# Two semaphore waits fewer on GpSimd in the scan stage of a recurrent-mix and slot-attention kernel

## The chip, the cores and the metric

The kernel runs on 1 core of one Trainium2 chip. The metric is the device time of one execution in microseconds (us), taken as a median over runs. The engines are named as the profile names them: PE is TensorE (PEld its weight loads), DVE is VectorE, ACT is ScalarE, POOL is GpSimd, SP is SyncE, whose queue carries the DMAs.

## The reference

Four sequences of 1024 steps and 1024 channels go through a two-way exponential-decay scan, then through two rounds of a slot-attention block. Only the scan part is touched by the change. In it, with k = v = the side input and r = x:

```python
decay = exp(-exp(w)) * (0.5 + 0.5 * tf)          # per sequence and channel
ek = exp(min(k, 30)); ekv = ek * v
# forward and backward over the steps: a = a * decay + ekv ; b = b * decay + ek
num = nf + nb - ekv + exp(min(u + k, 30)) * v
den = df + db - ek + exp(min(u + k, 30))
x0 = sigmoid(r) * (num / max(den, 1e-8)) * (0.8 + 0.2 * tf)
```

x0 then goes through the two rounds of normalisation, top-4 selection per slot, attention over 16 slots and output projection, and is added to x at the end.

## The kernel before

The scan stage works on 32 tiles (NT), one for each of 4 sequences and 8 groups of 128 channels; a tile is 128 partitions (channels) by 1024 steps in fp32, even steps in the first half of the columns and odd ones in the second. Each engine has one instruction stream written out by hand; the streams are tied by counting semaphores, `wait(engine, sem, count)`. A producer adds 1 to its semaphore for each instruction.

For tile i, in the order of the data:

- SP loads k into kbuf (two buffers) and r into rbuf (three). Line 230, the load of k for tile n + 2, waits for ekv_ok and euv_ok of tile n.
- POOL L347 writes min(k, 30) into ek (two buffers), a tensor_scalar.
- ACT L263 takes exp of ek in place (ek_ok).
- DVE L294 and L296 (the helper `halves`) join neighbouring steps of ek into gfk: each is a scalar_tensor_tensor on 512 columns that reads two halves of a tile in SBUF. They count prek_ok, two for each tile. DVE L302 and L305 (the helper `scans`) are the forward and the backward scan of gfk; their decay factor is in PSUM.
- POOL L351 is ekv = ek * k, a tensor_tensor of two SBUF tiles into the one buffer ekv. DVE L294 and L296 then run again, from ekv into gfv (prev_ok), and L302 and L305 again on gfv.
- ACT L283 makes eu = exp(u + k); DVE L330 makes euv from eu and kbuf, both in SBUF (euv_ok); DVE L334 adds eu and the PSUM sum to den (den_ok).
- PE (helper line L368) adds up the two scans in PSUM: 4 matmuls for num (num_ok), 4 for den (sumk_ok), 2 for euv. L391 transposes x0 and L405 makes logit sums.
- The quotient is taken in logarithms: ACT L276 and L278 on den (l2_ok), ACT L271 exp(-r) on rbuf, POOL L354 a cap on it (tensor_scalar, in place), ACT L287 its logarithm (l1_ok), POOL L360 the sum of the two (tensor_tensor, both inputs in SBUF, s_ok), ACT L246 the exp of it (y_ok), and DVE L325 multiplies it with num from PSUM.

DVE's order in iteration n is: halves of gfk(n), scans of gfk(n), halves of gfv(n), L325 of tile n - 1, L330(n), L334(n), scans of gfv(n). In the texts "halves of gfk" are L294 and L296 on ek, and "halves of gfv" the same lines on ekv. POOL's order in iteration i is L347(i), L351(i), L354(i), L360(i - 1). ACT's order in iteration i: L246(i - 2), L250(i - 3), L260(i), L263(i), L267(i - 2), L271(i), L276(i - 1), L278(i - 1), L283(i), L287(i).

Before the change, POOL L351(i) waits for three counts: ek_ok (ACT L263 of tile i), prev_ok (both halves of gfv of tile i - 1, which have read ekv), and euv_ok (DVE L330 of tile i - 1). POOL L360(i - 1) waits for l1_ok, l2_ok and for prek_ok of tile i, that is for the halves of gfk that DVE runs in iteration i.

Of the kernel before, what the change touches and what calls it, by code (L numbers as in the profile page):

```python
# [16 lines left out]
NT = B * NC  # L17
# [12 lines left out]
def wait(eng, sem, count):  # L30

    if not (isinstance(count, int) and count <= 0):
        eng.wait_ge(sem, count)
# [20 lines left out]
def build(nc, xT, kT, x, cond, w_cols, u_cols, work_t, cw_cols, npre_cols, cb_col, wr_T, wr_b, wq, wk_T,  # L54
          wv_T, bq_cols, bk_cols, bv_cols, wo_T, wo_b, npost, out):
    with ExitStack() as ctx:
# [56 lines left out]
        def csem(name):  # L113
            cond_sems.append(cond_ctx.enter_context(nc.semaphore(name)))
            return cond_sems[-1]
# [19 lines left out]
        def constants_pool(pool):  # L135

            nc.gpsimd.memset(ident[:], 0.0).then_inc(c_id, 1)
            nc.gpsimd.memset(fold[:], 0.0).then_inc(c_id, 1)
            nc.gpsimd.memset(ones_row, 1.0).then_inc(c_id, 1)
            pool.wait_ge(c_id, 3)  # L140
            nc.gpsimd.affine_select(out=ident[:], in_=ident[:], compare_op=ALU.not_equal, fill=1.0, base=0,
                                    pattern=[[-1, P]], channel_multiplier=1).then_inc(c_id, 1)
            for q in range(Q):
                nc.gpsimd.affine_select(out=fold[:], in_=fold[:], compare_op=ALU.not_equal, fill=1.0,
                                        base=-32 * q, pattern=[[-1, S]], channel_multiplier=1).then_inc(c_id, 1)
                pool.wait_ge(c_id, 5 + q)
# [64 lines left out]
        dg_ok, ekv_ok, euv_ok = csem("diag_ok"), csem("ekv_ok"), csem("euv_ok")  # L211
        prek_ok, prev_ok, gfk_ok, gfv_ok = csem("prek_ok"), csem("prev_ok"), csem("gfk_ok"), csem("gfv_ok")
# [5 lines left out]
        with nc.Block() as block:  # L218
            @block.sync
            def _(sp):  # L220
                constants_sp(sp)
                for n in range(NT):
                    p = n % 2
                    if n > 0:
                        wait(sp, x0_ok, n)
                        sp.dma_start(x0T_d[n - 1, :, :], x0T).then_inc(x0_out, 16)
                    if n + 2 < NT:
                        wait(sp, ekv_ok, n + 1)
                        wait(sp, euv_ok, n + 1)
                        sp.dma_start(kbuf[p], kT[n + 2, :, :]).then_inc(k_in[p], 16)  # L230
                    if n + 3 < NT:
                        wait(sp, s_ok, n + 1)
                        sp.dma_start(rbuf[n % 3], xT[n + 3, :, :]).then_inc(r_in[n % 3], 16)
                wait(sp, x0_ok, NT)
                sp.dma_start(x0T_d[NT - 1, :, :], x0T).then_inc(x0_out, 16)
                sp.wait_ge(x0_out, 16 * NT)
# [101 lines left out]
            @block.gpsimd  # L338
            def _(pool):
                constants_pool(pool)  # L340
                for i in range(NT + 1):
                    p = i % 2
                    if i < NT:
                        wait(pool, k_in[p], (i // 2 + 1) * 16)
                        wait(pool, prek_ok, 2 * (i - 1))
                        wait(pool, ekv_ok, i - 1)
                        nc.gpsimd.tensor_scalar(ek[p], kbuf[p], EXP_MAX, None, ALU.min).then_inc(kc_ok, 1)  # L347
                        wait(pool, ek_ok, i + 1)
                        wait(pool, prev_ok, 2 * i)
                        wait(pool, euv_ok, i)  # L350
                        nc.gpsimd.tensor_tensor(ekv, ek[p], kbuf[p], ALU.mult).then_inc(ekv_ok, 1)  # L351
                        r = rbuf[i % 3]
                        wait(pool, er_raw, i + 1)
                        nc.gpsimd.tensor_scalar(r, r, ER_CAP, None, ALU.min).then_inc(er_ok, 1)  # L354
                    if i > 0:
                        n = i - 1
                        wait(pool, l1_ok, n + 1)
                        wait(pool, l2_ok, n + 1)
                        wait(pool, prek_ok, 2 * min(i + 1, NT))
                        nc.gpsimd.tensor_tensor(den[n % 2], den[n % 2], rbuf[n % 3], ALU.add).then_inc(s_ok, 1)  # L360

            @block.tensor
# [808 lines left out]
```

## Time and profile before

| | before |
|---|---|
| median of 3 runs | 1146.97 us (1146.0 to 1147.72) |
| the profiled execution's own time | 1146.0 us |
| its span, first to last instruction | 1144.2 us |
| mean granted TensorE clock | 0.984 of full |
| scan stage | from the start to about 404 us |
| DVE busy from 200 to 300 us | 98.19 us |
| POOL busy from 200 to 300 us | 87.45 us |

The time lies 1.8 us above the span, for what is before the first and after the last instruction. The scan stage is the first 404 us, in which all engines work on 32 tiles in a pipeline with a fixed rhythm; the two rounds of attention follow. In a timeline row an instruction has its start, its duration, and in brackets how long its engine had been idle before it and what ended that idle time. Successive DVE instructions overlap by some 0.08 us in such rows: a start-to-start distance is that much shorter than the duration.

### The profile page before, as it was taken

The page shows a single profiled execution, that of the slowest core. Times are in us where ns is not written, and L with a number is a line of the kernel's source. Part 1 is how long each engine was busy: PE and PEld are TensorE (multiplying, and loading weights), DVE is VectorE, ACT ScalarE, POOL GpSimd, SP SyncE. Part 2 cuts the span into 40 slices and gives each one's busy share as a digit, 9 for nine tenths or more (in the row PEclk, how much of TensorE's full clock was granted, in tenths as well). Part 3 has the DMA queues.
Part 4 walks back from the last instruction along what each step waited for, and adds up shares of the span by engine and source line. Part 5 has one row for each costly group of instructions (what it writes and reads, how often), then busy time and mean ns, then how long its engine had stood idle before and what let it go on. Part 6 is the DMA issues. An engine that isn't in the chain of part 4 may idle for free. (4 is left out here: it accounts for less than half of the span.)

```text
span 1144.2 us, 15666 instructions
## 1 busy us (share of the span) xinstructions
PE 1060.2 (93%) x5040; PEld 587.0 (51%) x5040; DVE 782.6 (68%) x1018; ACT 595.5 (52%) x972; POOL 447.3 (39%) x204
## 2 busy tenths in 40 slices
PE   2999999999999978989999999998889899999996
PEld 1443434434344432646666666665326466666663
DVE  6999999999999832365665666655223666666664
ACT  4778787887877720245555555555202433333332
POOL 6889888898888600001111111111000023333333
PEclk9999999999999989999999999999799999999998
DMA  3343343433434174953345354331659656778764
GB/s 132 117 148 122 129 147 114 154 119 128 148 113 151 50 276 177 361 189 110 111 137 176 114 175 141 110 110 74 248 219 342 203 192 224 277 242 278 244 219 148
DMA packets 83392, 196.54 MB, mean 172 GB/s; under 512 B 6802, under 2 KB 48914, under 8 KB 80276
## 3 DMA queue, kind: packets, MB, share of 16 engines
q1 hardware_dynamic: 83348, 195.97, 48.9%
q8 instruction: 25, 0.41, 0.2%
q14 instruction: 19, 0.16, 0.0%
HBM read 137.22 MB, written 58.73 MB: 171 GB/s over the span
## 5 line engine op out<-in xcount | busy, mean ns | idle before, releaser
L929 PE MATMUL bank<-work 128*128 (+1 forms) x1024 | 247.7, 386 | 7.9 <-PEq L507 4.9
L953 PE MATMUL bank<-work 128*128 (+1 forms) x512 | 230.3, 592 | 2.6 <-ACT work L1053 1.8
L368 PE MATMUL bank<-work,ident 128*128 128x512 f32 x384 | 191.9, 622 | 33.8 <-DVE work L305 32.6
L929 PEld LDWEIGHTS bank<-work 128*128 128x128 f32 x1024 | 189.5, 192 | 46.8 <-issue 25.8
L1108 POOL TENSOR_TENSOR work<-work 128x1024 f32<-128x1024 f32 x32 | 75.4, 2357 | 263.6 <-DVE work L1035 263.6
L1098 POOL COPY xres<-work 128x1024 f32 (+1 forms) x32 | 33.3, 1041 | 369.6 <-DVE work L1035 369.6
L953 PEld LDWEIGHTS bank<-work 128*128 128x128 f32 x512 | 97.1, 190 | 98.0 <-issue 91.8
L368 PEld LDWEIGHTS bank<-work,ident 128*128 128x128 f32 x384 | 65.6, 190 | 127.2 <-issue 65.7
L987 DVE TENSOR_TENSOR work<-bank,sbias 128x256 f32<-128x256 f32 x64 | 27.2, 425 | 147.4 <-PE bank L929 147.4
L368 PE MATMUL bank<-work 128*128 128x511 f32 x256 | 120.1, 592 | 0.0
L347 POOL TENSOR_SCALAR work<-work 128x1024 f32<-128x1024 f32 x32 | 98.7, 3083 | 4.0 <-DMA work<-in_kT 1.4
L351 POOL TENSOR_TENSOR work<-work 128x1024 f32<-128x1024 f32 x32 | 76.0, 2375 | 45.9 <-DVE work L330 39.6
L354 POOL TENSOR_SCALAR work<-work 128x1024 f32<-128x1024 f32 x32 | 89.0, 2780 | 0.0
L1053 ACT ACTIVATE work<-bank 128x256 f32<-128x256 f32 x64 | 24.5, 383 | 123.2 <-PE bank L941 123.2
L1035 DVE SCALAR_TENSOR_TENSOR work<-work,stat 128x1024 f32<-128x1024 f32 x64 | 81.8, 1279 | 7.7 <-ACT stat L1061 7.7
L1020 DVE TENSOR_TENSOR work<-bank,xres 128x1024 f32<-128x1024 f32 x64 | 78.3, 1224 | 11.3 <-issue 7.7
L368 PEld LDWEIGHTS bank<-work 128*128 128x128 f32 x256 | 48.8, 191 | 61.6 <-issue 61.6
L1047 ACT ACTIVATE work<-work 128x256 f32<-128x256 f32 x64 | 26.7, 417 | 101.1 <-DVE work L992 101.1
L360 POOL TENSOR_TENSOR work<-work 128x1024 f32<-128x1024 f32 x32 | 75.5, 2359 | 9.5 <-issue 7.2
L302 DVE TENSOR_TENSOR_SCAN work<-bank,work 128x512 f32<-128x512 f32 x64 | 77.5, 1210 | 0.0
L305 DVE TENSOR_TENSOR_SCAN work<-bank,work 128x512 f32<-128x512 f32 x64 | 76.3, 1192 | 0.0
L296 DVE SCALAR_TENSOR_TENSOR work<-work,decay 128x512 f32<-128x512 f32 x64 | 71.5, 1118 | 0.0
(154 smaller groups left out, 1524.3 us busy)
## 6 DMA issues: line engine op xcount, KB each, us to landing
work<-in_kT SPq DMA_DIRECT2D x32, 512.0 KB, 3.5
work<-in_xT SPq DMA_DIRECT2D x32, 512.0 KB, 3.3
x0T_scratch<-work SPq DMA_DIRECT2D x32, 512.0 KB, 2.8
work<-x0T_scratch SPq DMA_DIRECT2D x32, 512.0 KB, 4.0
x1T_scratch<-work SPq DMA_DIRECT2D x32, 512.0 KB, 2.6
work<-x1T_scratch SPq DMA_DIRECT2D x32, 512.0 KB, 5.0
work<-in_x_nat SPq DMA_DIRECT2D x32, 512.0 KB, 4.5
out<-work SPq DMA_DIRECT2D x32, 512.0 KB, 3.0
```

Source lines behind the costliest of these rows:

```text
L302: nc.vector.tensor_tensor_scan(v[:, od], d2, v[:, od], 0.0, ALU.mult, ALU.add).then_inc(done, 1)
L305: nc.vector.tensor_tensor_scan(back, d2, back, 0.0, ALU.mult, ALU.add).then_inc(done, 1)
L347: nc.gpsimd.tensor_scalar(ek[p], kbuf[p], EXP_MAX, None, ALU.min).then_inc(kc_ok, 1)
L351: nc.gpsimd.tensor_tensor(ekv, ek[p], kbuf[p], ALU.mult).then_inc(ekv_ok, 1)
L354: nc.gpsimd.tensor_scalar(r, r, ER_CAP, None, ALU.min).then_inc(er_ok, 1)
L360: nc.gpsimd.tensor_tensor(den[n % 2], den[n % 2], rbuf[n % 3], ALU.add).then_inc(s_ok, 1)
L368: return nc.tensor.matmul(ps[:, at:at + n], w, v, start=start, stop=not start, skip_group_check=True)
L929: last = nc.tensor.matmul(ps_s[p], xTb[p][:, c, :], Amat[:, i, :, c * 32:c * 32 + 32], start=(c == 0), stop=(c == NC - 1))
L953: last = nc.tensor.matmul(ps_o[:, cols], attT[:, k * P:(k + 1) * P], Bmat[k][:, i, cols], start=(k == 0), stop=(k == 1), skip_group_check= ...
L1020: nc.vector.tensor_tensor(y.rearrange("p (c x) -> p c x", c=NC), ps_o[:, :].rearrange("p (c x) -> p c x", c=NC), xres[:, bass.ds(n // NC * ...
L1035: nc.vector.scalar_tensor_tensor(x1s[1 - p], y, stat[:, 2:3], npb, ALU.mult, ALU.mult)\
L1108: nc.gpsimd.tensor_tensor(x1s[p], x1s[p], xo[p], ALU.add).then_inc(fin, 1)
```

## The change

Two of POOL's waits are deleted. No instruction is added, removed or moved.

```diff
@@ -347,7 +347,6 @@
                         nc.gpsimd.tensor_scalar(ek[p], kbuf[p], EXP_MAX, None, ALU.min).then_inc(kc_ok, 1)
                         wait(pool, ek_ok, i + 1)
                         wait(pool, prev_ok, 2 * i)
-                        wait(pool, euv_ok, i)
                         nc.gpsimd.tensor_tensor(ekv, ek[p], kbuf[p], ALU.mult).then_inc(ekv_ok, 1)
                         r = rbuf[i % 3]
                         wait(pool, er_raw, i + 1)
@@ -356,7 +355,6 @@
                         n = i - 1
                         wait(pool, l1_ok, n + 1)
                         wait(pool, l2_ok, n + 1)
-                        wait(pool, prek_ok, 2 * min(i + 1, NT))
                         nc.gpsimd.tensor_tensor(den[n % 2], den[n % 2], rbuf[n % 3], ALU.add).then_inc(s_ok, 1)
```

L351 then waits for ek_ok and prev_ok alone, L360 for l1_ok and l2_ok alone. None of the four remaining counts is changed, and the buffers' safety does not hang on the deleted ones: ekv is free when prev_ok says so, and den and rbuf are touched by ACT alone before L360.

## Rows read from the trace of the kernel before

**Rows 1.** Page: busy us of each engine; and one DMA issue group.

```profile
PE 1060.2 (93%) x5040; PEld 587.0 (51%) x5040; DVE 782.6 (68%) x1018; ACT 595.5 (52%) x972; POOL 447.3 (39%) x204
...
work<-in_kT SPq DMA_DIRECT2D x32, 512.0 KB, 3.5
```

**Rows 2.** Windows: stretch, then busy us (count) by engine, PE clock, DMA.

```profile
200.00:300.00 100.00, 95.74 (x369) 40.61 (x367) 98.19 (x93) 79.92 (x86) 87.45 (x34) 1.00 0.39 138
```

**Rows 3.** Timeline of DVE in the steady rhythm: start, us, instruction.

```profile
201.73 1.21 DVE L330 SCALAR_TENSOR_TENSOR work<-work 128x1024 f32<-128x1024 f32 x1
...
202.86 1.21 DVE L334 SCALAR_TENSOR_TENSOR work<-work,bank 128x1024 f32<-128x1024 f32 x1
...
203.99 1.21 DVE L302 TENSOR_TENSOR_SCAN work<-bank,work 128x512 f32<-128x512 f32 x1
...
205.13 1.19 DVE L305 TENSOR_TENSOR_SCAN work<-bank,work 128x512 f32<-128x512 f32 x1
...
206.24 0.80 DVE L294 SCALAR_TENSOR_TENSOR work<-work,decay 128x512 f32<-128x512 f32 x1
...
206.96 0.74 DVE L296 SCALAR_TENSOR_TENSOR work<-work,decay 128x512 f32<-128x512 f32 x1
...
207.62 1.21 DVE L302 TENSOR_TENSOR_SCAN work<-bank,work 128x512 f32<-128x512 f32 x1
...
208.76 1.19 DVE L305 TENSOR_TENSOR_SCAN work<-bank,work 128x512 f32<-128x512 f32 x1
...
210.18 0.91 DVE L294 SCALAR_TENSOR_TENSOR work<-work,decay 128x512 f32<-128x512 f32 x1 [0.23 <-PE bank L368]
...
211.01 1.52 DVE L296 SCALAR_TENSOR_TENSOR work<-work,decay 128x512 f32<-128x512 f32 x1
...
212.46 1.27 DVE L325 SCALAR_TENSOR_TENSOR work<-bank,gain,work 128x1024 f32<-128x1024 f32 x1
...
213.65 1.21 DVE L330 SCALAR_TENSOR_TENSOR work<-work 128x1024 f32<-128x1024 f32 x1
```

**Rows 4.** Timeline of POOL in the same stretch.

```profile
203.12 2.37 POOL L351 TENSOR_TENSOR work<-work 128x1024 f32<-128x1024 f32 x1 [1.32 <-DVE work L330]
...
205.46 2.76 POOL L354 TENSOR_SCALAR work<-work 128x1024 f32<-128x1024 f32 x1
...
208.19 2.35 POOL L360 TENSOR_TENSOR work<-work 128x1024 f32<-128x1024 f32 x1
...
210.62 3.09 POOL L347 TENSOR_SCALAR work<-work 128x1024 f32<-128x1024 f32 x1
```

**Rows 5.** Timeline of ACT and PE in the same stretch.

```profile
201.83 1.06 ACT L263 ACTIVATE work<-work 128x1024 f32<-128x1024 f32 x1 [0.92 <-POOL work L347]
...
208.20 1.88 PE L368 MATMUL bank<-work 128*128 128x511 f32 x4
```

**Rows 6.** Timeline of DVE in the first two tiles.

```profile
12.08 2.87 DVE L294 SCALAR_TENSOR_TENSOR work<-work,decay 128x512 f32<-128x512 f32 x1 [1.49 <-ACT work L263]
14.87 1.52 DVE L296 SCALAR_TENSOR_TENSOR work<-work,decay 128x512 f32<-128x512 f32 x1
...
24.09 1.22 DVE L334 SCALAR_TENSOR_TENSOR work<-work,bank 128x1024 f32<-128x1024 f32 x1 [3.02 <-PE bank L368]
...
27.48 0.73 DVE L294 SCALAR_TENSOR_TENSOR work<-work,decay 128x512 f32<-128x512 f32 x1
28.12 0.75 DVE L296 SCALAR_TENSOR_TENSOR work<-work,decay 128x512 f32<-128x512 f32 x1
```

**Rows 7.** Timeline of POOL in the first two tiles.

```profile
12.05 2.35 POOL L351 TENSOR_TENSOR work<-work 128x1024 f32<-128x1024 f32 x1 [5.11 <-ACT work L263]
14.37 3.21 POOL L354 TENSOR_SCALAR work<-work 128x1024 f32<-128x1024 f32 x1
...
29.04 2.35 POOL L360 TENSOR_TENSOR work<-work 128x1024 f32<-128x1024 f32 x1 [2.38 <-DVE work L296]
```

**Rows 8.** Timeline of ACT in the second tile.

```profile
26.53 1.15 ACT L278 ACTIVATE work<-work,tiny 128x1024 f32<-128x1024 f32 x1
```

## The prediction

> **What bounds the kernel now.** I read the page first [rows 1], where the reader is to see which engine looks idle: PE is busiest over the whole, POOL with 39% looks idle. That average says nothing here, because POOL's work of this change lies in the first 404 us alone. The windows show it: between 200 and 300 us DVE is busy for 98.19 of 100 us, at full granted clock, with POOL at 87.45 [rows 2]. The timeline then gives the rhythm. L330 starts at 201.73 and again at 213.65 [rows 3]: one tile takes 11.92 us, and DVE has one gap in it, 0.23 us in front of L294 at 210.18. So DVE sets this stage's pace, and the question is what stretches DVE's instructions.
>
> Two of them are stretched. L294 and L296 are 512-column instructions that take 0.72 to 0.75 us when nothing disturbs them [rows 3, 6], but the halves of gfv take 0.91 and 1.52 us. L296 at 211.01 lies under POOL's L347, which itself takes 3.09 us where the same operation at 205.46 took 2.76 [rows 4]. The start of the stage shows the thing undiluted: POOL's L351 starts at 12.05 and takes 2.35; DVE's L294 starts 0.03 us later and takes 2.87 us, that is 2.15 more than alone, and ends at 14.95, one undisturbed duration after L351's last 0.2 us [rows 6, 7]. Scans (L302, L305) under L351 and L360 take the usual 1.2 us. From these rows I take this mechanism of the kernel:
>
> - DVE's L294, L296 and L330 (two SBUF inputs) and POOL's instructions exclude each other.
> - A POOL tensor_tensor (L351, L360) keeps such a DVE instruction out for its whole duration less some 0.17 us: 2.15 to 2.20 us. L360, 208.19 to 210.54, explains the 0.91 of L294 at 210.18 in the same way.
> - A POOL tensor_scalar (L347, L354) keeps it out only at its start: L354 starts at 205.46, yet L294 at 206.24 takes 0.80 and the next L296 0.74. The exclusion is about 0.86 us from its start, or 0.78 from when it is let in.
> - When POOL waits while L294 runs, POOL is let in before the L296 that follows: L347 waited 0.33 us for L294 and then L296 waited 0.78; the same at 14.37 with L354 (3.21 us) and L296 (1.52) [rows 6, 7].
>
> The Trainium skill, page "SBUF — State Buffer", section "Who interferes with whom", says that a DVE instruction with two SBUF inputs contends with a GpSimd instruction that reads SBUF, and that the first to issue holds the shared port for its whole instruction. For the tensor_tensors the rows agree (2.15 of 2.35 us); for L354 they do not: by the rule L294 at 206.24 would have waited until 208.22, 1.98 us, and it lost 0.08. Used on the sum below, which blocks on tensor_tensors only, rule and rows give the same time.
>
> **The change, part by part.** No work is removed, so both deletions count only by what POOL does earlier.
>
> *The euv_ok wait, steady rhythm.* L351 at 203.12 is released by L330, which ended at 202.94; L263, its other producer, ended at 202.89 [rows 3 to 5]. The 1.32 us of idle time are therefore almost all needed anyway: the gain lies between 0 and 0.23 us a tile (it can't start before 202.89). I take 0.10, as the handover after L330 took 0.18 and one from ACT may take a little less. That holds as long as POOL's chain is not ahead of DVE.
>
> *The prek_ok wait, steady rhythm.* L360 at 208.19 follows L354 at once, after the halves of gfk (206.24 to 207.70). The wait is not what holds it: nothing gained. But it held once: at 29.04, after 2.38 us of idle time, released by L296 [rows 7]. The early start of the first L360 decides the case, so I follow it.
>
> *Tile 1 without the waits.* L278 of tile 0 ends at 26.53 + 1.15 = 27.68 [rows 8]; L360(0) is ready at about 27.76. DVE's L294 runs from 27.48 to 28.21, so L360 waits and, by the fourth point, gets in before L296 (due 28.12). L296 is held for 2.19 us, to 30.31. It was 28.12 before. L360 ends near 30.5, L347(2) starts near 30.6, waits for L296 (until about 31.0) and ends at about 33.75; L263(2) ends 1.09 later at 34.85; L351(2) could start at 34.93. Its other wait, prev_ok: DVE goes on 30.31 + 0.66 + 1.13 + 1.12 = 33.22 (L294 of gfv), 33.86 (L296, ends 34.60), 34.52 (L325), 35.71 (L330). So L351(2) starts 0.8 us ahead of L330(1), where euv_ok would have placed it after. L330 is held until 34.93 + 2.19 = 37.12, 1.4 us.
>
> *Does it repeat?* Then L334 starts at 37.12 + 1.13 = 38.25. In tile 0, from L334's start (24.09) to L278's end (27.68) it is 3.59 us, so L360 is ready 3.67 after L334's start; DVE's L294 of gfk comes 3.38 after it (203.99 to 206.24 in the rows is L302, L305: 206.24 − 202.86 = 3.38) and L296 0.64 later, at 4.02. L360(1) arrives between the two, 0.35 us before L296, if POOL's L354 is over by then. It is: L354(2), behind L271, starts near 37.9, is held by L330 until 38.25, and ends near 41.0; L360 is ready at 41.9. Before, L354 ended 5.3 us after L334's start and hid this. So L296 is blocked again, and the rhythm feeds itself: L360 blocks L296 of gfk, L351 blocks L330, and DVE, being late, leaves POOL ahead.
>
> *The period.* DVE undisturbed, start to start: L294 0.64, L296 0.66, L302 1.13, L305 1.12, L294 0.64, L296 0.66, L325 1.19, L330, L334 and L302 1.13 each, L305 1.12 = 10.55 us [rows 3, 6]. (The same loop now: 10.55 + 0.97 for the halves of gfv + 0.08 for L294 + 0.30 for PE = 11.90.) In the new rhythm POOL's L347 comes 2.4 us after L360 was let in and is past its exclusive part before the halves of gfv, so these are free; and PE's four matmuls of num, 3.7 us up to 208.20 + 1.88 = 210.08 [rows 5], are over before DVE's longer way through gfk (0.64 + 2.19 + 0.66 + 1.13 + 1.12 = 5.74), so that gap closes. Period = 10.55 + 2.19 + 1.39 = 14.13 us, 2.21 more than now.
>
> *What else waits.* L354 is behind L351 on POOL; L287 and L246 on ACT wait for POOL, and L325 for L246: L246 would be done 1.1 us after L360 ends, some 3 us ahead of L325. SP's load of k (line 230) still waits for both ekv and euv and lands in 3.5 us [rows 1], with more time than now. None sets the end.
>
> *The sum.* L294(2) now starts 14 periods before that of tile 16, at 206.24 − 14 × 11.92 = 39.36; it moves to 38.25 + 3.38 = 41.63: +2.3. Then 29 periods to L294(31), 29 × 2.21 = +64.1. In tile 31 L296 is blocked once more but the PE gap is closed, 5.74 against 3.94: +1.8; its gfv half is no longer blocked, −0.2. Nothing in the attention stages changes. Together +68.0 us. On the profiled execution's 1146.0 us that is 1214.0; its time is 0.97 us under the median of the runs shown, so 1215.0.
>
> Bounds of the unknown costs: the block by a tensor_tensor is 2.15 to 2.20; L351's lead over L330 is between 0.8 and 0.93 (it needs prev_ok, 0.18 after L296's end), so L330 loses 1.22 to 1.40. The period is then 13.92 to 14.15 us and the sum +62 to +69: 1209 to 1216, and I allow 1204 to 1222 for handovers that no row shows.
>
> **The rivals.**
>
> *The blocked rhythm never starts, time falls.* If DVE keeps the port across L294 and L296 when a tensor_tensor waits, or L360(0) comes 0.4 us later, L360(0) starts at about 28.8 and everything is as before, with L351 up to 0.23 us earlier each tile. At 0.10 × 30 = 3 us: 1144 (1140 to 1147). For it: the priority is shown only with tensor_scalars as the waiting instruction. Against: it is the same queue and port, and it fell so at 14.87 and again in the steady rhythm at 211.01 [rows 3, 6]. It decides at one point, 28.12 us.
>
> *One block, then recovery.* L360(0) blocks L296 once, +2.4 us, but L360(1) comes after L296 (0.35 us of margin): POOL gets back behind DVE. With 0 to 3 us gained on the rest: 1147 to 1150. Against it: the 3.67 and 4.02 us hang on durations that repeat within 0.02 us.
>
> *Half of it.* Only L296 is held each tile, and L351 comes after L330: the period is 10.55 + 2.19 = 12.74, +0.82 in each of 29 tiles, 24, and +4 for the first and the last: 1175. Or both are held, but by less than the full duration: up to 1204. For it: L351's time hangs on a chain of four handovers on POOL and ACT; against: it would have to slip by 0.8 us.
>
> *The waits were never binding, no change.* True of both in the steady rhythm, and so it would be if the start were as now; that is the first rival with a gain of 0.
>
> **How the numbers follow.** The blocked rhythm 0.70; half of it 0.08; one block 0.05; never started 0.17, of which 0.10 gains more than 2.3 us. The difference that a measurement of this kernel can tell from none is about 0.2%, 2.3 us. The predicted time is that of the likeliest, 1215. The range goes from the lower end of the half case, 1168, to the top of the likeliest, 1222; the likeliest's own range is 1204 to 1222. Faster 0.10; same 0.07 + 0.03 = 0.10; slower 0.80.
>
> **What would show it.** In the timeline after: L360(0) near 27.8 us, and the L296 behind it at 2.9 us; from then on, in each tile, one L296 of 2.9 and an L330 of 2.6 us, L296 of gfv back at 0.74, L330 to L330 14.1 us; the scan stage ending near 472 instead of 404; DVE still busy over 95% of it, PE down to about 80%. The prediction is wrong if L296 at 28.12 still takes 0.75 us, or if L330 stays at 1.21.

## The result, and the profile after

| | before | after |
|---|---|---|
| median | 1147.05 us (4 runs) | 1219.07 us (1218.29 to 1219.74, 4 runs) |
| the profiled execution's own time | 1146.0 us | 1219.75 us |
| its span | 1144.2 us | 1217.9 us |
| mean granted TensorE clock | 0.984 | 0.971 |

The ratio is 1.0628, with a 95% interval of 1.061 to 1.0647: slower by 72 us, where 68 were forecast (1215, range 1168 to 1222).

After the change the numbers of later lines fall by one behind the first deletion and by two behind the second: L351 becomes L350, L354 L353, L360 L358. The head, the parts of the page and of its costliest groups (mean of one in ns, then idle time before them), next to [rows 1]:

```profile
span 1217.9 us, 15666 instructions
...
PE 1069.4 (88%) x5040; PEld 594.0 (49%) x5040; DVE 855.5 (70%) x1018; ACT 598.8 (49%) x972; POOL 463.0 (38%) x204
...
L296 DVE SCALAR_TENSOR_TENSOR work<-work,decay 128x512 f32<-128x512 f32 x64 | 113.4, 1772 | 0.0
...
L358 POOL TENSOR_TENSOR work<-work 128x1024 f32<-128x1024 f32 x32 | 82.9, 2592 | 49.8 <-ACT work L278 49.8
...
L330 DVE SCALAR_TENSOR_TENSOR work<-work 128x1024 f32<-128x1024 f32 x32 | 79.5, 2485 | 0.0
```

DVE's busy time grew by 72.9 us (782.6 to 855.5) with the same 1018 instructions, which is nearly the whole loss of 73.75 us in the profiled execution. A wait that was deleted came back as busy time of another engine: a blocked instruction counts as busy. A reader who looks only for idle gaps misses it: in the scan stage DVE's waits for PE come to 14.3 us before and to 14.2 us after.

The start, in the timelines of DVE and POOL of the changed kernel, next to [rows 6, 7]:

```profile
28.49 0.73 DVE L294 SCALAR_TENSOR_TENSOR work<-work,decay 128x512 f32<-128x512 f32 x1
29.13 2.85 DVE L296 SCALAR_TENSOR_TENSOR work<-work,decay 128x512 f32<-128x512 f32 x1
...
36.65 2.57 DVE L330 SCALAR_TENSOR_TENSOR work<-work 128x1024 f32<-128x1024 f32 x1
...
28.84 2.60 POOL L358 TENSOR_TENSOR work<-work 128x1024 f32<-128x1024 f32 x1 [2.04 <-ACT work L278]
...
35.78 2.36 POOL L350 TENSOR_TENSOR work<-work 128x1024 f32<-128x1024 f32 x1 [1.17 <-ACT work L263]
```

POOL's sum (L358) is issued 0.35 us into L294, waits for its end, and is let in ahead of L296, which takes 2.85 us instead of 0.75. Then L350 starts 0.87 us ahead of L330, which takes 2.57 instead of 1.21. The whole start lies 1.0 us later than before for another reason, below. The rhythm that follows, in the same kernel's timelines of DVE and POOL, next to [rows 3, 4]:

```profile
221.45 2.57 DVE L330 SCALAR_TENSOR_TENSOR work<-work 128x1024 f32<-128x1024 f32 x1
223.94 1.21 DVE L334 SCALAR_TENSOR_TENSOR work<-work,bank 128x1024 f32<-128x1024 f32 x1
...
227.32 0.72 DVE L294 SCALAR_TENSOR_TENSOR work<-work,decay 128x512 f32<-128x512 f32 x1
227.96 2.85 DVE L296 SCALAR_TENSOR_TENSOR work<-work,decay 128x512 f32<-128x512 f32 x1
...
220.57 2.36 POOL L350 TENSOR_TENSOR work<-work 128x1024 f32<-128x1024 f32 x1 [1.17 <-ACT work L263]
223.65 2.99 POOL L353 TENSOR_SCALAR work<-work 128x1024 f32<-128x1024 f32 x1 [0.71 <-ACT work L271]
227.66 2.60 POOL L358 TENSOR_TENSOR work<-work 128x1024 f32<-128x1024 f32 x1 [1.02 <-ACT work L278]
```

Both blocks recur in every tile; only L330 of the last tile, which no L350 follows, is free. L358 is issued 3.72 us after L334 starts; L296 comes 4.02 us after it. Start to start, L296 now holds DVE for 2.77 us instead of 0.66 (2.11 more) and L330 for 2.49 instead of 1.13 (1.36 more), so the undisturbed 10.55 us become 14.02.

One thing was not in the forecast. Ten of the tiles took some 14.6 us instead of 14.03. The timeline of the changed kernel, DVE and PE, and then the windows of two like stretches (PE clock is the third number from the end):

```profile
209.90 1.22 DVE L334 SCALAR_TENSOR_TENSOR work<-work,bank 128x1024 f32<-128x1024 f32 x1 [0.49 <-PE bank L366]
...
204.47 3.40 PE L366 MATMUL bank<-work,ident 128*128 128x512 f32 x4 [1.97 <-DVE work L305]
...
219.08 1.98 PE L366 MATMUL bank<-work,ident 128*128 128x512 f32 x4 [1.96 <-DVE work L305]
```

```profile
204.30:210.00 5.70, 5.54 (x11) 2.47 (x12) 5.21 (x6) 3.06 (x3) 3.82 (x3) 0.70 0.23 92
218.90:224.60 5.70, 5.10 (x17) 2.67 (x18) 5.70 (x6) 3.06 (x3) 3.82 (x3) 1.00 0.24 95
```

In the first stretch the granted clock was 0.70 on average, so part of it was spent at 1.2 and not at 2.4 GHz; four matmuls took 3.40 us instead of 1.98, and L334 waited for their sum. DVE waited so 10 times after the start, 6.4 us in all: nine times 0.5 us, and 1.85 us in tile 31. Before the change the clock's mean was 1.00 between 200 and 300 us [rows 2], and also over the first 404 us.

### The profile page after: what moved, and what is told of

Its sections match the earlier page's. It is cut to its first block and busy times, and to the rows that moved or that the text cites. A ratio compares the mean times of both kernels' runs of the same rounds, so it can differ in the third digit from the quotient of the medians.

```text
span 1217.9 us, 15666 instructions
## 1 busy us (share of the span) xinstructions
PE 1069.4 (88%) x5040; PEld 594.0 (49%) x5040; DVE 855.5 (70%) x1018; ACT 598.8 (49%) x972; POOL 463.0 (38%) x204
## 5 line engine op out<-in xcount | busy, mean ns | idle before, releaser
L366 PE MATMUL bank<-work,ident 128*128 128x512 f32 x384 | 200.8, 648 | 98.8 <-DVE work L305 89.8
L927 PEld LDWEIGHTS bank<-work 128*128 128x128 f32 x1024 | 188.4, 191 | 47.0 <-issue 26.5
L1106 POOL TENSOR_TENSOR work<-work 128x1024 f32<-128x1024 f32 x32 | 75.4, 2358 | 263.1 <-DVE work L1033 263.1
L951 PEld LDWEIGHTS bank<-work 128*128 128x128 f32 x512 | 97.7, 191 | 99.2 <-issue 92.9
L366 PE MATMUL bank<-work 128*128 128x511 f32 x256 | 128.6, 627 | 0.0
L296 DVE SCALAR_TENSOR_TENSOR work<-work,decay 128x512 f32<-128x512 f32 x64 | 113.4, 1772 | 0.0
L353 POOL TENSOR_SCALAR work<-work 128x1024 f32<-128x1024 f32 x32 | 95.9, 2996 | 21.4 <-ACT work L271 21.4
L358 POOL TENSOR_TENSOR work<-work 128x1024 f32<-128x1024 f32 x32 | 82.9, 2592 | 49.8 <-ACT work L278 49.8
L347 POOL TENSOR_SCALAR work<-work 128x1024 f32<-128x1024 f32 x32 | 98.2, 3070 | 3.9 <-DMA work<-in_kT 1.3
L350 POOL TENSOR_TENSOR work<-work 128x1024 f32<-128x1024 f32 x32 | 75.6, 2363 | 41.6 <-ACT work L263 41.6
L366 PEld LDWEIGHTS bank<-work 128*128 128x128 f32 x256 | 53.4, 209 | 70.0 <-issue 70.0
L330 DVE SCALAR_TENSOR_TENSOR work<-work 128x1024 f32<-128x1024 f32 x32 | 79.5, 2485 | 0.0
```

The lines of the kernel that those rows point to most:

```text
L296: nc.vector.scalar_tensor_tensor(dst[:, ev], src[:, od], d, src[:, ev], ALU.mult, ALU.add)\
L330: nc.vector.scalar_tensor_tensor(euv, eu[p], EXP_CAP, kbuf[p], ALU.min, ALU.mult)\
L366: return nc.tensor.matmul(ps[:, at:at + n], w, v, start=start, stop=not start, skip_group_check=True)
L927: last = nc.tensor.matmul(ps_s[p], xTb[p][:, c, :], Amat[:, i, :, c * 32:c * 32 + 32], start=(c == 0), stop=(c == NC - 1))
L951: last = nc.tensor.matmul(ps_o[:, cols], attT[:, k * P:(k + 1) * P], Bmat[k][:, i, cols], start=(k == 0), stop=(k == 1), skip_group_check= ...
```

## The experiments

Theory A: without the two waits the stage has two rhythms that keep themselves going, one in which POOL is behind DVE (11.8 us a tile) and one in which it is ahead and blocks it twice a tile (14.03 us); the start chooses the second. The main rival, B: each deleted wait costs its own share in every tile. Every kernel below is the changed one with the edit shown. Medians stand beside those of the kernel before on the same chip.

**One wait back at a time.** First the wait of L351 is put back:

```diff
                         wait(pool, prev_ok, 2 * i)
+                        wait(pool, euv_ok, i)
```

> Only the wait for prek_ok is deleted; the one for euv_ok is back. Theory A (the blocked rhythm feeds itself and needs both waits gone): L360 of tile 0 blocks the halves of gfk of tile 1 once (L296 2.85 us), then L351 is held behind L330, POOL falls back behind DVE, and the period returns to 11.92 us: 1148 to 1150 us, one or two long L296. Rival B (each deleted wait costs its own share in every tile): L296 at 2.85 us in each tile, 2.11 x 31 = 65 us less what closes of gaps: about 1190 to 1210 us.

Measured: 1147.2 us beside 1148.54, ratio 1.0004 (0.9987 to 1.0021), 0.8 us under the expected range. Its timelines of DVE and POOL:

```profile
28.88 2.85 DVE L296 SCALAR_TENSOR_TENSOR work<-work,decay 128x512 f32<-128x512 f32 x1
...
36.40 1.21 DVE L330 SCALAR_TENSOR_TENSOR work<-work 128x1024 f32<-128x1024 f32 x1
...
41.80 0.75 DVE L296 SCALAR_TENSOR_TENSOR work<-work,decay 128x512 f32<-128x512 f32 x1
...
37.78 2.38 POOL L351 TENSOR_TENSOR work<-work 128x1024 f32<-128x1024 f32 x1 [3.43 <-DVE work L330]
```

L296 is blocked once, in tile 1. Then L351 idles for 3.43 us until L330 is done, and that throws POOL back behind DVE: the next L296 takes 0.75 us. Now the other wait alone:

```diff
                         wait(pool, l2_ok, n + 1)
+                        wait(pool, prek_ok, 2 * min(i + 1, NT))
```

> Only the wait for euv_ok is deleted; the one for prek_ok is back. Theory A: the start is as before, POOL stays behind DVE, no L330 is blocked; L351 starts with L263's release instead of L330's, some 0.1 us earlier in each tile: 1143 to 1146 us, period about 11.82. Rival B: L330 at 2.57 us in each tile, 1.36 x 31 = 42 us: about 1175 to 1190 us.

Measured: 1143.23 us, ratio 0.996 (0.9944 to 0.9975): 0.4% faster than the kernel before. No L330 takes over 1.214 us. Its timelines of DVE and POOL:

```profile
198.56 1.52 DVE L296 SCALAR_TENSOR_TENSOR work<-work,decay 128x512 f32<-128x512 f32 x1
...
210.34 1.52 DVE L296 SCALAR_TENSOR_TENSOR work<-work,decay 128x512 f32<-128x512 f32 x1
...
202.44 2.38 POOL L350 TENSOR_TENSOR work<-work 128x1024 f32<-128x1024 f32 x1 [1.17 <-ACT work L263]
```

The period is 11.78 us, 0.14 less than 11.92; POOL's product is released by ACT's exp and idles for 1.17 us instead of 1.32 [rows 4]. Rival B falls: alone, the one deletion costs nothing that can be measured and the other gains.

**Only the start guarded.**

```diff
+                        if i == 1:
+                            wait(pool, prek_ok, 2 * min(i + 1, NT))
```

> Both waits are deleted, but the very first L360 (tile 0) keeps its wait for prek_ok. Theory A: the start decides; without the first block POOL never gets ahead, and all 31 tiles run at about 11.82 us: 1143 to 1147 us, no L296 at 2.85 but the one of tile 0. Rival B: 30 of 31 tiles run without either wait and cost as in the changed kernel: 1215 to 1219 us.

Measured: 1143.3 us, ratio 0.9963 (0.995 to 0.9977). One wait, executed once, takes away the whole loss; the other 31 tiles run without either and show no L296 over 1.53 us.

**One wait in the middle.** No wait but that of L351 in tile 16:

```diff
+                        if i == 16:
+                            wait(pool, euv_ok, i)
```

> Both waits are deleted, but L351 of tile 16 alone keeps its wait for euv_ok. Theory A: the blocked rhythm starts at tile 1 and is broken once, at tile 16: tiles 2 to 15 at 14.03 us and more, those after 17 at about 11.8: about half of the loss, 1178 to 1185 us. Rival B: one wait of 32 brings back 1 to 3 us: 1215 to 1218 us.

Measured: 1179.2 us beside 1148.54, ratio 1.0268 (1.024 to 1.0296): a loss of 31 us instead of 72. The timelines of DVE and POOL at the place:

```profile
226.90 2.85 DVE L296 SCALAR_TENSOR_TENSOR work<-work,decay 128x512 f32<-128x512 f32 x1
...
234.43 1.21 DVE L330 SCALAR_TENSOR_TENSOR work<-work 128x1024 f32<-128x1024 f32 x1
...
239.82 0.75 DVE L296 SCALAR_TENSOR_TENSOR work<-work,decay 128x512 f32<-128x512 f32 x1
...
235.81 2.38 POOL L352 TENSOR_TENSOR work<-work 128x1024 f32<-128x1024 f32 x1 [3.43 <-DVE work L330]
```

From there on all tiles are of the short kind. One of the four executions took 1217.76 us, about the time of the changed kernel; it has no trace, and whether the wait failed to break the rhythm, something set it going again, or it has another cause is open.

**The other way round: DVE is made late once.** L334 of tile 16 runs three times in a row, in the kernel that guards only the start and in the one that keeps the prek_ok wait throughout:

```diff
+                        for j in range(2 if n == 16 else 0):
+                            nc.vector.scalar_tensor_tensor(den[p], eu[p], EXP_CAP, ps_den[:, :], ALU.min, ALU.add)\
+                                .then_inc(again, 1)
+                            wait(dve, again, j + 1)
                         nc.vector.scalar_tensor_tensor(den[p], eu[p], EXP_CAP, ps_den[:, :], ALU.min, ALU.add)\
```

> The kernel with the one wait at the start (only the first L360 waits for prek_ok), in which DVE runs L334 of tile 16 three times, so that it comes about 2.3 us late once. Theory A (two rhythms, both self-keeping without the waits): L360 of tile 16 gets in ahead of L296, and tiles 17 to 31 run at about 14.03 us: 1176 to 1184 us. Rival B (the good rhythm restores itself): the 2.3 us and no more, 1144 to 1148 us.

> The same disturbance (L334 of tile 16 three times) in the kernel that keeps the prek_ok wait in all tiles and has only the euv_ok wait deleted. Theory A: the wait keeps L360 behind the halves of gfk, the rhythm recovers in the next tile, and the cost is what was added: 1144 to 1147 us. Rival B (the remaining wait does not protect L330): 1176 to 1184 us.

Measured: 1180.84 us (ratio 1.029, 1.0263 to 1.0317) for the unguarded, 1145.91 us (0.9985, 0.997 to 1.0001) for the guarded one. The unguarded kernel's timelines of DVE and POOL:

```profile
218.72 0.73 DVE L295 SCALAR_TENSOR_TENSOR work<-work,decay 128x512 f32<-128x512 f32 x1
219.36 2.85 DVE L297 SCALAR_TENSOR_TENSOR work<-work,decay 128x512 f32<-128x512 f32 x1
...
226.88 2.57 DVE L331 SCALAR_TENSOR_TENSOR work<-work 128x1024 f32<-128x1024 f32 x1
...
219.06 2.60 POOL L365 TENSOR_TENSOR work<-work 128x1024 f32<-128x1024 f32 x1 [1.00 <-ACT work L279]
```

and the guarded one's:

```profile
219.77 0.74 DVE L297 SCALAR_TENSOR_TENSOR work<-work,decay 128x512 f32<-128x512 f32 x1
...
220.69 2.36 POOL L364 TENSOR_TENSOR work<-work 128x1024 f32<-128x1024 f32 x1 [2.23 <-DVE work L297]
```

2.5 us of lateness cost 37.5 us without the wait (1180.84 against 1143.3 for the same kernel undisturbed) and about 2.7 us with it (1145.91 against 1143.23); the kernels compared ran on different chips, so the last digits are not exact. In the guarded kernel the wait holds L364 in that one tile, 2.23 us, and at the start of the stage, 2.82 us; in no other tile.

**What blocks whom.** L360's tensor_tensor becomes a tensor_scalar; the addition of log(1 + exp(-r)) is left out:

```diff
-                        nc.gpsimd.tensor_tensor(den[n % 2], den[n % 2], rbuf[n % 3], ALU.add).then_inc(s_ok, 1)
+                        nc.gpsimd.tensor_scalar(den[n % 2], den[n % 2], BIG, None, ALU.min).then_inc(s_ok, 1)
```

> Both waits are deleted; L360's tensor_tensor (den + log r) is replaced by a tensor_scalar with one input (a minimum with 3e38), so the addition of log(1 + exp(-r)) is left out. Theory A (a GpSimd tensor_tensor keeps the halves out for 2.1 us, a tensor_scalar only for its first 0.8 us): L296 of gfk loses 0.8 us at most where it meets L360, L330 is not blocked any more, and the period is about 11.9 to 12.0 although the new instruction takes 2.76 us and not 2.35: 1146 to 1151 us. Rival B (any GpSimd instruction holds the port for its whole duration): L296 is held for 2.5 us or more, period above 14: 1220 to 1235 us.

Measured: 1152.32 us beside 1146.92, ratio 1.0043 (1.0026 to 1.006), 1.3 us above the expected range. Its timelines of POOL and DVE, first where the changed kernel tips over, then in the steady rhythm:

```profile
28.83 3.00 POOL L358 TENSOR_SCALAR work<-work 128x1024 f32<-128x1024 f32 x1 [2.07 <-ACT work L278]
29.12 1.52 DVE L296 SCALAR_TENSOR_TENSOR work<-work,decay 128x512 f32<-128x512 f32 x1
...
196.54 2.77 POOL L353 TENSOR_SCALAR work<-work 128x1024 f32<-128x1024 f32 x1
...
196.89 1.23 DVE L294 SCALAR_TENSOR_TENSOR work<-work,decay 128x512 f32<-128x512 f32 x1
198.05 0.74 DVE L296 SCALAR_TENSOR_TENSOR work<-work,decay 128x512 f32<-128x512 f32 x1
...
203.28 1.28 DVE L325 SCALAR_TENSOR_TENSOR work<-bank,gain,work 128x1024 f32<-128x1024 f32 x1 [0.94 <-ACT work L246]
```

The replaced instruction, at the same place as before (0.35 us into L294), now costs L296 0.78 us and not 2.11. In the steady rhythm L294 starts 0.35 us into another tensor_scalar (L353) and loses 0.51 us: the exclusion ends 0.86 us after the tensor_scalar's start, and L296 runs freely under its rest. The period, 12.1 us, is now set by POOL's own longer loop (L325 waits 0.94 us for it), which the expectation had put 0.1 us too short.

Next the DVE side: L296 of gfk takes its second tensor from PSUM, so gfk's even half holds another value. Then all five two-input instructions do, L330 among them (gfk, gfv and euv hold other values). The edit shown is that of the first kernel.

```diff
-                    nc.vector.scalar_tensor_tensor(dst[:, ev], src[:, od], d, src[:, ev], ALU.mult, ALU.add)\
+                    nc.vector.scalar_tensor_tensor(dst[:, ev], src[:, od], d,
+                                                   src[:, ev] if second is None else second,
+                                                   ALU.mult, ALU.add)\
...
-                        halves(gfk, ek[p], d, prek_ok)
+                        halves(gfk, ek[p], d, prek_ok, decay2[:, n:n + 1].broadcast_to([P, HT]))
```

> Both waits are deleted; in the halves of gfk, L296's second tensor is read from PSUM (the decay column, broadcast) and not from the even half of ek in SBUF, so gfk's even half holds another value. Nothing else moves. Theory A (the exclusion is between GpSimd and an instruction with two SBUF inputs): L296 takes 0.74 us under L360, the blocked rhythm never starts: 1142 to 1146 us. Rival B (L296 is slow under L360 whatever it reads, or waits for something else): 1215 to 1220 us as in the changed kernel.

> Both waits are deleted; all five DVE instructions with two SBUF inputs (L294 and L296 twice, L330) read their second tensor from PSUM, a broadcast decay column, so gfk, gfv and euv hold other values. Theory A: no exclusion is left, L296 takes 0.74, L330 1.21, L294 0.72, L347 2.76 us; then GpSimd's own loop (L347 2.77, L263 1.1, L351 2.33, L354 2.73, L360 2.43) sets the period, about 11.4: 1130 to 1136 us. Rival B (the collisions are no matter of the second SBUF input): 1215 to 1220 us.

Measured, beside 1146.92: 1141.18 us (ratio 0.994, 0.9919 to 0.9962), 0.8 us under the expected range, and 1131.73 us (0.9867, 0.9838 to 0.9897). The first kernel's timelines of DVE and POOL at the place where the changed kernel tips over:

```profile
26.69 0.72 DVE L294 SCALAR_TENSOR_TENSOR work<-work,decay 128x512 f32<-128x512 f32 x1
27.33 0.74 DVE L296 SCALAR_TENSOR_TENSOR work<-work,decay,bank 128x512 f32<-128x512 f32 x1
...
27.03 2.60 POOL L360 TENSOR_TENSOR work<-work 128x1024 f32<-128x1024 f32 x1 [0.20 <-ACT work L278]
```

POOL's sum comes at the same point as in the changed kernel, 0.34 us into L294, and L296 runs under it in 0.74 us. The column read in place of the tile is broadcast, so it is also a smaller read; a full tile from PSUM does not collide either, as L335 of the next kernel shows. In the second, POOL's own loop sets the pace at 11.46 us, as its rows of L325 (here L327) and L347 (here L350) show: DVE waits for POOL's chain through ACT, and L350 is back at 2.77 us.

```profile
201.79 1.28 DVE L327 SCALAR_TENSOR_TENSOR work<-bank,gain,work 128x1024 f32<-128x1024 f32 x1 [0.41 <-ACT work L246]
...
213.25 1.28 DVE L327 SCALAR_TENSOR_TENSOR work<-bank,gain,work 128x1024 f32<-128x1024 f32 x1 [0.41 <-ACT work L246]
...
212.21 2.77 POOL L350 TENSOR_SCALAR work<-work 128x1024 f32<-128x1024 f32 x1
```

**Another order on DVE.** L330 moves ahead of L325, right behind the halves of gfv:

```diff
+                    if n < NT:
+                        wait(dve, eu_ok, n + 1)
+                        wait(dve, euv_used, n)
+                        nc.vector.scalar_tensor_tensor(euv, eu[p], EXP_CAP, kbuf[p], ALU.min, ALU.mult)\
+                            .then_inc(euv_ok, 1)
                     if n > 0:
                         wait(dve, y_ok, n)
...
-                        wait(dve, eu_ok, n + 1)
-                        wait(dve, euv_used, n)
-                        nc.vector.scalar_tensor_tensor(euv, eu[p], EXP_CAP, kbuf[p], ALU.min, ALU.mult)\
-                            .then_inc(euv_ok, 1)
```

> Both waits are deleted; DVE runs L330 (euv) ahead of L325 (the quotient), right behind the halves of gfv, so that it starts before L351 can. Theory A: one block of L296 at the start, but L330 takes 1.21 us and keeps L351 back instead, POOL stays behind DVE, period 11.8 to 11.9: 1143 to 1150 us. Rival B (the blocked rhythm needs only L296 against L360): L296 at 2.85 us in each tile, 1180 to 1215 us.

Measured: 1148.25 us beside 1146.92, ratio 0.9999 (0.9981 to 1.0016); one of its ten executions took 5784.57 us, for which no trace shows a reason. Its timelines of DVE (L321 is the moved instruction, L335 the one that was L334) and POOL:

```profile
203.59 1.29 DVE L294 SCALAR_TENSOR_TENSOR work<-work,decay 128x512 f32<-128x512 f32 x1 [0.67 <-PE bank L367]
...
205.47 1.21 DVE L321 SCALAR_TENSOR_TENSOR work<-work 128x1024 f32<-128x1024 f32 x1
...
207.79 1.20 DVE L335 SCALAR_TENSOR_TENSOR work<-work,bank 128x1024 f32<-128x1024 f32 x1
...
207.24 2.38 POOL L351 TENSOR_TENSOR work<-work 128x1024 f32<-128x1024 f32 x1 [1.17 <-ACT work L263]
```

L335, with one input in SBUF and a full tile in PSUM, starts 0.55 us into POOL's L351 and takes 1.20 us. L296 is blocked in tiles 1 and 2 (2.85 us each), once more than expected: in between L335 waited 1.85 us for PE, so DVE was late again. From tile 3 on L296 takes 0.74 us. With L330 out of L351's reach the blocked rhythm thus dies out without any wait: the block of L296 alone does not keep POOL ahead, here and with the euv_ok wait back. Whether the block of L330 alone would is not shown: in no kernel did it occur without the other. Against the kernel before nothing is gained: the collision of L347 with the halves of gfv stays (L294 at 1.29 us).

**The clock.** 12 extra matmuls fill the time in which PE waits for gfk's scans; the wait for den_ok moves ahead of them:

```diff
+                        wait(pe, den_ok, n)
+                        for j in range(12 if n > 0 else 0):
+                            nc.tensor.matmul(ps_den[:, 0:P], ident[:], ident[:], start=True, stop=True,
+                                             skip_group_check=True)
                         wait(pe, gfk_ok, 2 * n + 2)
                         wait(pe, dg_ok, n + 1)
-                        wait(pe, den_ok, n)
```

> Both waits are deleted; in each tile but the first PE runs 12 extra 128x128 matmuls into the den sums' first columns, which the next matmul overwrites, in the 1.97 us in which it waits for gfk's scans. Theory C (the 10 waits of L334 for PE, 6.4 us in all, come from stretches in which the granted clock had fallen after PE had stood idle): with the gap filled the clock stays at 1.00 in the stage, no L334 waits, the period is 14.03 in every tile: 1211 to 1215 us. Rival D (the clock falls for something else, or the filler delays den): 1218 us or more.

Measured: 1213.12 us beside 1147.8, ratio 1.0561 (1.0536 to 1.0587), some 6 us under the changed kernel's 1219.07 (which was measured at another time, so the difference is not exact). Its windows:

```profile
100.00:200.00 100.00, 97.25 (x482) 54.50 (x481) 100.00 (x78) 68.49 (x73) 79.01 (x30) 1.00 0.30 111
200.00:300.00 100.00, 97.25 (x492) 55.21 (x491) 100.00 (x80) 69.28 (x74) 79.11 (x29) 1.00 0.33 115
```

More work on PE made the kernel faster: the clock stays at 1.00, DVE is busy for all of the 100 us, and the waits of L334 after the start fall from 6.4 us in 10 to 0.6 us in one, in tile 31. No tile takes over 14.06 us. In the changed kernel's stage the profile shows the drop only after the 1.97 us gaps, but not after each of them; which gaps bring it was not found out.

## Why the prediction was right

Point by point, by its own steps:

- *The mechanism.* The exclusion between DVE's two-input instructions and POOL, taken from [rows 3, 4, 6, 7], is shown: it goes away when the second input is in PSUM (1131.73 us with none left), and the tensor_scalar holds only its first 0.86 us, measured again at 196.89. The Trainium skill, page "SBUF — State Buffer", section "Who interferes with whom", which says that the first to issue holds the port for its whole instruction, agrees with the tensor_tensors (2.11 us of L296 in each tile); for the tensor_scalars the runs decide otherwise, 0.51 us lost at 196.89 in the kernel with the one-input sum, where the rule would give 2.4.
- *Who is let in.* That POOL's waiting instruction goes ahead of the next L296 was known only for tensor_scalars. It held for the tensor_tensor at 28.84 us and in each tile after. In all of them POOL's instruction was issued some 0.3 us before L296, so the runs do not tell a priority of POOL from first come, first served.
- *The steady rhythm without the first collision.* The euv_ok wait was put at 0.10 us a tile, between 0 and 0.23; it was 0.14. That the prek_ok wait gains nothing there is shown by 11.78 us in both kernels that lack the euv_ok wait, with the other and without it.
- *The start decides, and the rhythm feeds itself.* Shown by the one guarded L360 (1143.3), by the one wait at tile 16 (1179.2) and by the one late tile (1180.84).
- *The rivals.* "Never starts" is what the kernels do that keep the prek_ok wait, in all tiles or in the first, and "one block, then recovery" what the one does that keeps the euv_ok wait; the changed kernel does neither. The measured place of L360 after L334 was 3.72 us, where 3.67 was worked out, with 0.30 us of margin to L296.

The sum, in the profiled execution, where 68.0 us were forecast and its time grew by 73.75:

| term | forecast | measured |
|---|---|---|
| start, up to L334 of tile 0 | 0 | +1.0 (25.10 against 24.09) |
| tile 1 | +2.3 | +2.3 |
| 29 periods | +64.1 (14.13 each) | +61.2 (14.03 each) |
| slow stretches of PE in them | 0 | +5.0 |
| tile 31 | +1.6 | +1.6, and +1.85 for one wait for PE |
| what follows, the attention stages above all | 0 | +0.8 |

The period was 0.10 us too long because the block by a tensor_tensor is 2.11 us on L296 and not 2.19, and 1.36 on L330 and not 1.39. What was missing is PE: the clock of 1.00 in [rows 2] was carried over to a rhythm in which PE stands idle for 2 us in each tile. Of the 1.85 us in tile 31, 0.6 us remain with the clock at 1.00, as the kernel with the extra matmuls shows: there L334, no longer behind a blocked L330, comes too early for PE's sum. The 1.0 us at the start has no part in the change: PE's first matmuls began 0.1 us later and took 0.9 us longer in this execution, and among the ten kernels whose first tile is the same L334 of tile 0 begins anywhere from 24.06 to 25.63 us.

## What to carry to other kernels

A wait that guards no data can guard a rhythm: before deleting one, look in the trace for what it holds apart, and follow the pipeline from its first tile, since a wait that binds once in 32 tiles (2.38 us here) can be worth 72 us. Where DVE sets the pace, its instructions with two SBUF inputs and POOL's tensor_tensors are to be kept apart by data waits or by a second input in PSUM, and the sign of trouble is a longer mean duration at an unchanged count, not idle time. Of the two waits either one was enough: with the euv_ok wait alone the time is as before, and with the prek_ok wait alone the kernel is 0.4% faster and also stands one late tile.

## What the runs showed of the hardware

- A POOL tensor_scalar of 128x1024 in fp32, 2.77 us long, keeps a two-input DVE instruction out only for 0.86 us after its start; a tensor_tensor of 2.36 us for 2.1 to 2.2 us.
- A POOL instruction that is issued while L294 runs is let in ahead of the L296 behind it, in 31 of 31 tiles; a second DVE input in PSUM takes the collision away (L296 0.74 us under a tensor_tensor instead of 2.85).
- PE's granted clock fell to a mean of 0.70 over 5.7 us in some tiles with idle gaps of 1.97 us, and not in others with the same gaps; matmuls for no purpose in those gaps took some 6 us off the kernel.
- Not all of it repeats from execution to execution: the same program with one wait in tile 16 took 1177.1 to 1179.41 us in three executions and 1217.76 in a fourth, for which there is no trace.
